# Eight-stage transformer kernel on one core: the wide attention's queries turned by VectorE 32x32 squares and a DRAM round trip instead of by TensorE, its probabilities divided on GpSimd, the narrow attention's copies moved to ScalarE, and a new order of steps

## Chip, cores and metric

One NeuronCore of a Trainium2 chip runs the whole program. The metric is device time in microseconds of one execution. All arithmetic the prediction speaks of is float32, except where a shape says f16 or bf16.

## What is computed

Four layers over x of 16x128x256, that is 16 blocks of 128 rows (context 128 rows of 128 a block), each layer a cross-attention and a feed-forward part, both added to x after a layer norm:

```python
x = x + _L0_xattn_ref(ln(x), ...)   # 32 heads of 8, rotary angles         -> stage 0
x = x + _L0_ffn_ref(ln(x), ...)     # product-key expert retrieval          -> stage 1
x = x + _L1_xattn_ref(ln(x), ...)   # 16 heads of 128, masked, grouped      -> stage 2
x = x + _L1_ffn_ref(ln(x), ...)     # 7 routed experts and a shared one     -> stages 3, 8, 9
x = x + _L2_xattn_ref(ln(x), ...)   # 16 heads of 16, two softmaxes, biases -> stage 4
x = x + _L2_ffn_ref(ln(x), ...)     # ternary weights                       -> stage 5
x = x + _L3_xattn_ref(ln(x), ...)   # 16 heads of 128, normed q and k       -> stage 6
x = x + _L3_ffn_ref(ln(x), ...)     # block-quantised weights and inputs    -> stage 7
```

The wide attention of layer 3 is `q = rmsnorm(x@Wq, gq); k = rmsnorm(ctx@Wk, gk); p = softmax(q k^T / sqrt(128)); out = (p v) @ Wo`, for 16 heads of 128.

## The kernel before

Every block of 128 rows passes through the steps listed in `STEPS`. Each step has a name, a number of repeats (4 in stage 6: four groups of four heads) and the engines that work on it (T TensorE, V VectorE, A ScalarE, G GpSimd, S the sync engine that issues DMAs). `ORDER` is a string per engine, one letter a step, that lays down by hand in which order the engine runs all its steps; the stages overlap at their borders, and stage 7 runs interleaved with stage 6, stage 1 with the end of stage 0, stage 5 with stage 4. Every engine works strictly in its order and waits on semaphores. Eight PSUM banks of 128x512 are handed round by `BANKS`.

Stage 6, per group of four heads (64 groups in all). TensorE: `q` (L1301, L1302) and `k` (L1308) project; `tq` (L1314) turns the four queries with four transposes into a PSUM bank; `sc` (L1323) makes scores; `pv` (L1329) and `wo` (L1337) follow. ScalarE: `q` copies the queries out of PSUM (L1644) and squares them (L1647), `k` squares the keys (L1652), `tq` copies the turned queries with the gain (L1658), `sc` is the exponential (L1673), `pv` a copy (L1664). VectorE: `nk`, `nq` sum the squares (L2313, L2319), `kn` scales the keys (L2324), `tk` turns them in 32x32 squares (L2333), `sc` takes the maximum (L2347) and scales it (L2351), `pn` takes the reciprocal of the sums (L2356) and multiplies the 128x512 probabilities by it (L2358), `pt` turns these in squares (L2341). GpSimd: the powers of -1/2 of `nk` and `nq` (L2564 to L2572), and one DMA each for `tk` (L2555) and `pt` (L2560), which writes the squares to DRAM. The sync engine then reads them back with four DMAs of 64 KB each, so placed that the squares land where a full 128x128 turn wants them (`turned_in`, L866). Keys and probabilities already take this way; queries don't. Stage 7 has VectorE steps on 128x1024 tiles (L2368 to L2420).

Stage 0: `split` makes the low halves of the f16 pairs with two subtractions on VectorE (L1867, L1868), while GpSimd duplicates the high halves (L2525, L2526); GpSimd also adds the rotary terms (L2520) and the output bias (L2515).

Stage 4: VectorE takes the turned keys out of PSUM with weight and bias (L1878, L1879), and the values with side mask and bias (L1899, twice a block); ScalarE takes the queries (L1451). A step `ms` interleaves on TensorE the maximum-squares of block b with the score-squares of block b-1 (L1016, L1012), two banks each; GpSimd raises the variances to -1/2 (L2533).

The way of keys and probabilities through DRAM, in the code:

```python
eng.dma_start(turn3k[n % 4], u6.Dk.rearrange("p (j w) -> p j w", j=4)).then_inc(S["l3_kw"], 16)   # GpSimd
src = mem.rearrange("(i r) j w -> i r j w", i=4)                                                   # sync engine
for j in range(4):
    eng.dma_start(to[32 * j:32 * j + 32].rearrange("r (i w) -> r i w", i=4), src[:, :, j, :].rearrange("i r w -> r i w")).then_inc(done, 16)
```

## Time and profile before

| | |
|---|---|
| time, median of 3 runs | 2078.17 us (2077.08 to 2088.37) |
| the profiled execution | 2088.02 us, its span 2085.8 us, mean granted TensorE clock 0.989 |
| busy, share of the span | TensorE 96%, weight loads 75%, VectorE 82%, ScalarE 61%, GpSimd 32% |
| chain that ended last | TensorE 53%, VectorE 29%, issue 7%, ScalarE 4%, GpSimd 4%, DMA 3% |

Busy is a union of recorded durations. Matmuls are pipelined and their records overlap, so a busy TensorE may still have room. The chain of waits is followed back from the last instruction, at each step to what released it. Lines of stage 6 are L1301 to L1337 (TensorE), L1644 to L1673 (ScalarE) and L2313 to L2358 (VectorE).

### The profile page before, as it was taken

How to read it: one execution, taken by the hardware profiler on the slowest of the kernel's cores; microseconds unless marked ns; L12 is line 12 of the kernel's file. 1: busy time of each engine (PE TensorE's matmuls, PEld its weight loads, DVE VectorE, ACT ScalarE, POOL GpSimd, SP SyncE). 2: the span in 40 equal slices, each digit the busy share in tenths (PEclk: the TensorE clock that was granted, in tenths of full speed). 3: DMA queues.
4: the chain of work that ended last, by engine and by line, in shares of the span. 5: the costliest groups of instructions: out<-in, count | busy, mean ns of one | idle time of the engine just before them, and what ended most of it. 6: DMA issues, size and time to landing. Idle time of an engine off the chain costs nothing.

```text
span 2085.8 us, 46042 instructions
## 1 busy us (share of the span) xinstructions
PE 1997.6 (96%) x16294; PEld 1564.6 (75%) x16294; DVE 1713.2 (82%) x4655; ACT 1274.0 (61%) x3214; POOL 667.7 (32%) x1000
## 2 busy tenths in 40 slices
PE   5999899999999999998998889999999999999998
PEld 3666799999988888877997667887665666656665
DVE  7887899999689997766447789896887998888877
ACT  3778988798944554544653444634766666567552
POOL 6321020000012232222128776111665345434420
PEclk8999999999999999999999899999999999999999
DMA  9400300000045443433220010023544233333320
GB/s 336 144 3 2 124 6 2 2 2 2 12 151 168 137 151 104 142 102 89 89 65 26 29 62 2 2 87 122 166 150 133 91 112 114 127 105 107 122 81 25
DMA packets 181515, 182.28 MB, mean 87 GB/s; under 512 B 20678, under 2 KB 160088, under 8 KB 180264
## 3 DMA queue, kind: packets, MB, share of 16 engines
q1 hardware_dynamic: 160168, 112.49, 17.5%
q0 software_dynamic: 21120, 66.87, 8.8%
q8 instruction: 130, 2.13, 0.4%
q14 instruction: 97, 0.79, 0.1%
HBM read 99.06 MB, written 80.22 MB: 86 GB/s over the span
## 4 chain that ended last, share of the span: by engine, by line
PE 53%; DVE 29%; issue 7%; ACT 4%; POOL 4%; DMA 3%; SPq 1%; another core or an unknown queue 0%; DVEq 0%; ACTq 0%; POOLq 0%
PE pb L1141 4%; PE pb L1164 3%; PE pb L1274 3%; PE pb L1337 2%; PE pb L1042 2%; PE pb L1149 2%; PE pb L1376 2%; PE pb L1359 2%; PE pb L1222 2%; PE pb L1360 2%; PE pb L1156 2%; PE pb L1283 2%; PE pb L995 2%; PE pb L1213 2%; PE pb L1329 1%
## 5 line engine op out<-in xcount | busy, mean ns | idle before, releaser
L2472 POOL TENSOR_SCALAR sm<-sm 128x1 f32<-128x1 f32 x128 | 33.7, 263 | 455.9 <-DVE sm L1745 454.9
L1508 ACT ACTIVATE areaB<-i128h,workB 128x128 f16<-128x128 f16 x512 | 156.2, 392 | 0.1
L1465 ACT ACTIVATE areaA<-pb 128x512 f32<-128x512 f32 x192 | 106.8, 600 | 61.6 <-PE pb L1012 35.2
L1535 ACT ACTIVATE workA<-workA 128x128 f32<-128x128 f32 x256 | 99.4, 390 | 60.8 <-DVE workA L2059 55.5
L1673 ACT ACTIVATE workA<-pb,workA 128x128 f32<-128x128 f32 x256 | 113.9, 460 | 30.9 <-DVE workA L2351 30.3
L1097 PE MATMUL pb<-areaB 128*128 128x128 f32 x1024 | 126.7, 280 | 3.1 <-ACT workB L1498 2.9
L1141 PE MATMUL pb<-xT,areaA 128*128 128x128 f32 x1024 | 124.2, 276 | 0.0
L1097 PEld LDWEIGHTS pb<-areaB 128*128 128x128 f32 x1024 | 119.8, 194 | 5.6 <-ACT workB L1498 3.3
L1141 PEld LDWEIGHTS pb<-xT,areaA 128*128 128x128 f32 x1024 | 120.0, 192 | 4.5 <-issue 4.0
L1164 PE MATMUL pb<-areaA,workA 128*128 128x256 f32 x512 | 121.6, 382 | 0.9 <-ACT workA L1542 0.9
L1337 PE MATMUL pb<-areaA,workA 128*128 128x256 f32 x512 | 120.7, 380 | 0.0
L2541 POOL DMA_DIRECT2D turn<-workA x64 | 37.1, 580 | 245.3 <-DVE workA L2072 244.8
L1113 PE MATMUL pb<-areaB,workB 128*128 128x256 f32 x512 | 113.7, 380 | 1.1 <-DVE workB L2036 1.1
L1337 PEld LDWEIGHTS pb<-areaA,workA 128*128 128x128 f32 x512 | 95.0, 190 | 25.3 <-issue 12.9
L1164 PEld LDWEIGHTS pb<-areaA,workA 128*128 128x128 f32 x512 | 93.8, 190 | 21.6 <-issue 8.5
L1113 PEld LDWEIGHTS pb<-areaB,workB 128*128 128x128 f32 x512 | 96.0, 190 | 13.9 <-DVE workB L2036 1.3
L1887 DVE TENSOR_REDUCE workA<-pb 128x4 f16<-128x512 f32 x128 | 83.4, 689 | 13.9 <-PE pb L995 13.5
L1042 PE MATMUL pb<-areaA,workA 128*32 128x128 f32 (+1 forms) x1536 | 86.4, 285 | 5.3 <-ACT areaA L1465 4.3
L2533 POOL TENSOR_TENSOR areaA<-areaA,neghalf 128x32 f32<-128x32 f32 x16 | 87.6, 5475 | 1.3
L1323 PEld LDWEIGHTS pb<-workA 128*128 128x128 f32 x512 | 65.1, 191 | 21.7 <-issue 18.6
L2474 POOL TENSOR_TENSOR sm<-sm,neghalf 128x1 f32<-128x1 f32 x128 | 76.7, 599 | 10.7
L1664 ACT COPY workA<-pb 128x512 f32<-128x512 f32 x64 | 37.8, 590 | 66.5 <-PE pb L1329 66.0
(426 smaller groups left out, 5872.0 us busy)
## 6 DMA issues: line engine op xcount, KB each, us to landing
turn<-workA POOLq DMA_DIRECT2D x64, 256.0 KB
workA<-turn SPq DMA_DIRECT2D x256, 64.0 KB
turn3k<-areaA POOLq DMA_DIRECT2D x64, 256.0 KB, 2.7
workA<-turn3k SPq DMA_DIRECT2D x256, 64.0 KB, 2.0
turn3p<-areaA POOLq DMA_DIRECT2D x64, 256.0 KB, 2.7
rows_in<-areaB SPq DMA_DIRECT2D x7, 2048.0 KB, 16.5
areaA<-turn3p SPq DMA_DIRECT2D x168, 64.0 KB, 2.0
workA<-turn3p SPq DMA_DIRECT2D x88, 64.0 KB, 2.0
```

The lines of the kernel that those rows point to most:

```text
L1042: m = eng.matmul(p[r, k * 128:(k + 1) * 128], vt[:, h, :], P[:, j * 128:(j + 1) * 128], start=True, stop=True)
L1097: m = eng.matmul(p[:, e * 128:(e + 1) * 128], w.ed[:, k, (4 * c + e) * 128:(4 * c + e + 1) * 128], xT[:, k, :], start=(k == 0), stop=(k == 1))
L1113: m = eng.matmul(p[:, 0:256], G[:, e, :], w.eu[:, e, :], start=(e == 0), stop=(e == 15))
L1141: m = eng.matmul(p[:, h * 128:(h + 1) * 128], w.wq[:, 4 * c + h, k], xT[:, k, :], start=(k == 0), stop=(k == 1))
L1164: m = eng.matmul(p[:, 0:256], u.OT[i][:, h], w.wo[:, 4 * c + h], start=(c == 0 and h == 0), stop=(c == 3 and h == 3))
L1337: m = eng.matmul(p[:, 0:256], u.OT[i][:, h], w.wo[:, 4 * c + h], start=(c == 0 and h == 0), stop=(c == 3 and h == 3))
L1465: eng.activation(u.P[n % RP], bank(*held)[:, :], ACT.Exp, scale=1.0 / math.sqrt(hd)).then_inc(freed(*held)[0], 1)
L1508: m = eng.activation(u.far[:, g], i128h[:, :], ACT.Square, bias=u.at[b % 2][:, 8 * c + g:8 * c + g + 1])
L1535: m = eng.activation(u.P[i][:, h], u.P[i][:, h], ACT.Exp, accum_out=u.den[i][:, h:h + 1], bias=u.nm[i][:, h:h + 1])
L1673: m = eng.activation(u.P[i][:, h], p[:, h * 128:(h + 1) * 128], ACT.Exp, accum_out=u.den[i][:, h:h + 1], bias=u.nb[i][:, h:h + 1], scale=u ...
L1887: eng.tensor_reduce(o[:, :, 24:25], p, AX.X, ALU.max, negate=True).then_inc(freed(s, tag, b, c // 2)[0], 1)
L2533: eng.tensor_tensor(va, va, neghalf[:, 0:32], ALU.pow).then_inc(S["l2_rs"], 1)
```

## The change

- Stage 6, queries: TensorE's `tq` and ScalarE's copy (L1644) go. VectorE turns the queries in squares straight from PSUM; GpSimd writes them to DRAM with one DMA; the sync engine reads them back with four; ScalarE applies the gain from SBUF; `sc` waits for that. ScalarE's square of the queries now waits for VectorE's squares, and `q` alternates between two banks (0 and 3).
- Stage 6, probabilities: VectorE keeps the reciprocal, GpSimd multiplies the 128x512 tile.
- Stage 0: the two subtractions of `split` run on GpSimd, behind its copies.
- Stage 4: ScalarE takes the turned keys and the values; the value bias leaves that step and is added, both sides summed, in `oT`, which becomes two activations with bias instead of a copy. `ms` is split into `mx` and `st`, each over four row groups and the same four banks (3 to 6); TensorE's matmuls are the same.
- `ORDER` is new for all five engines. The stages overlap about as before: at its last step of stage 0 VectorE has 33 steps of stage 1 behind it, where it had 24; at the last step of stage 5 it has 16 of stage 6, where it had 14.

The core of the diff (the order strings, names of semaphores, buffers of stage 4 and the host's preparation of the bias are left out):

```diff
-    0: (("lnA", 1, "VG"), ("lnB", 1, "VG"), ("xT", 1, "TA"), ("qk", 1, "T"), ("rope", 1, "VG"), ("split", 1, "AVG"),
+    0: (("lnA", 1, "VG"), ("lnB", 1, "VG"), ("xT", 1, "TA"), ("qk", 1, "T"), ("rope", 1, "VG"), ("split", 1, "AG"),
-        ("nc", 1, "V"), ("tqk", 1, "TAV"), ("vp", 1, "TV"), ("ms", 2, "T"), ("mxr", 4, "V"), ("tq2", 1, "TA"),
-        ("ex", 4, "A"), ("pv", 4, "T"), ("ot", 2, "A"), ("tb", 2, "T"), ("norm", 2, "V"), ("oT", 1, "TA"),
+        ("nc", 1, "V"), ("tqk", 1, "TA"), ("vp", 1, "TA"), ("mx", 1, "T"), ("mxr", 4, "V"), ("tq2", 1, "TA"),
+        ("st", 1, "T"), ("ex", 4, "A"), ("pv", 4, "T"), ("ot", 2, "A"), ("tb", 2, "T"), ("norm", 2, "V"), ("oT", 1, "TA"),
-    6: (("lnA", 1, "VG"), ("lnB", 1, "V"), ("xT", 1, "TA"), ("k", 4, "TA"), ("nk", 4, "VG"), ("kn", 4, "V"), ("q", 4, "TA"),
-        ("nq", 4, "VG"), ("tq", 4, "TA"), ("tk", 4, "VGS"), ("sc", 4, "TVA"), ("pn", 4, "V"), ("pt", 4, "VGS"),
+    6: (("lnA", 1, "VG"), ("lnB", 1, "V"), ("xT", 1, "TA"), ("k", 4, "TA"), ("nk", 4, "VG"), ("kn", 4, "V"), ("q", 4, "TVA"),
+        ("nq", 4, "VG"), ("tq", 4, "GSA"), ("tk", 4, "VGS"), ("sc", 4, "TVA"), ("pn", 4, "VG"), ("pt", 4, "VGS"),
...
-    (6, "q"): lambda b, c: (("q", 0),),
+    (6, "q"): lambda b, c: (("q", (0, 3)[c % 2]),),
-        u6.qn = [carve(512) for _ in range(2)]
+        u6.Dq = [carve(512) for _ in range(2)]
         u6.qT = [carve(512).rearrange("p (h n) -> p h n", n=128) for _ in range(2)]
+        u6.qr = [work[1][:, 8704 + 512 * k:9216 + 512 * k] for k in range(2)]
         u6.kT = [carve(512) for _ in range(2)]
...
+                elif (s, step) == (6, "tq"):
+                    n = 4 * b + c
+                    d.wait_ge(S[f"l3_qw{n % 2}"], 16 * (n // 2 + 1))
+                    if n >= 2:
+                        d.wait_ge(S["l3_qg"], n - 1)
+                    turned_in(turn3q[n % 4], u6.qr[n % 2], S[f"l3_qr{n % 4}"])
...
+                    rows = range(2 * (c % 2), 2 * (c % 2) + 2) if s == 0 else range(4)
+                    tags = [step + "ab"[i % 2] if s == 0 else f"{step}{i}" for i in rows]
+                    p = [room(s, tag, b, c) for tag in tags]
...
-                elif step == "tq":
-                    t.wait_ge(S["l3_qn"], nth(b, c, 4))
-                    p = room(6, "tq", b, c)
-                    for h in range(4):
-                        m = eng.transpose(p[:, h * 128:(h + 1) * 128], u.qn[i][:, h * 128:(h + 1) * 128], ident)
-                    m.then_inc(full(6, "tq", b, c)[0], 1)
...
+                        if step == "tqk":
+                            a.wait_ge(*full(4, "tk", b))
+                            src, dst = bank(4, "tk", b)[:, :].rearrange("p (t n) -> p t n", n=128), u.kT[b % RQ]
+                            eng.activation(dst[:, :, 0:112], src[:, :, 0:112], ACT.Identity, scale=w4.nwc[:, 1:2], bias=w4.nwc[:, 4:5])
+                            eng.activation(dst[:, :, 112:128], src[:, :, 112:128], ACT.Identity, scale=w4.nwc[:, 2:3],
+                                           bias=w4.nwc[:, 5:6]).then_inc(freed(4, "tk", b)[0], 1)
...
+                    src = bank(4, "v", b)[:, 0:256].rearrange("p (h e) -> p h e", e=16)
+                    for k in range(2):
+                        m = eng.activation(u.vt[b % RV][:, :, 17 * k:17 * k + 16], src, ACT.Copy, scale=side[k])
...
+                        for k in range(2):
+                            m = eng.activation(u.OT[b % 2][:, k], src[:, k], ACT.Identity, bias=w4.bsum[:, k:k + 1])
...
                 elif step == "q":
                     a.wait_ge(*full(6, "q", b, c))
-                    p = bank(6, "q", b, c)
-                    if two:
-                        a.wait_ge(*full(6, "tq", *two))
-                    eng.copy(u.qn[i], p[:, :]).then_inc(S["l3_qn"], 1)
+                    a.wait_ge(S["l3_qt"], nth(b, c, 4))
                 elif step == "tq":
-                    a.wait_ge(*full(6, "tq", b, c))
+                    n = 4 * b + c
+                    a.wait_ge(S["gp_done"], 1)
+                    a.wait_ge(S[f"l3_qr{n % 4}"], 64 * (n // 4 + 1))
-                    a.wait_ge(S["gp_done"], 1)
-                    eng.activation(u.qT[i], bank(6, "tq", b, c)[:, :].rearrange("p (h n) -> p h n", h=4), ACT.Copy,
-                                   scale=gp[:, 0:1]).then_inc(freed(6, "tq", b, c)[0], 1)
+                    eng.activation(u.qT[i].rearrange("p h (i w) -> p h i w", i=4),
+                                   u.qr[i].rearrange("p (i h w) -> p h i w", i=4, h=4), ACT.Copy, scale=gp[:, 0:1]).then_inc(S["l3_qg"], 1)
...
-                    eng.tensor_tensor(qp[:, 0, :, 8:16], y4[:, 0], qp[:, 0, :, 0:8], ALU.subtract)
-                    eng.tensor_tensor(qp[:, 1, :, 16:24], y4[:, 1], qp[:, 1, :, 0:8], ALU.subtract).then_inc(S["l0_split"], 1)
...
-                        eng.tensor_scalar(dst[:, :, 0:112], src[:, :, 0:112], w.nwc[:, 1:2], w.nwc[:, 4:5], ALU.mult, ALU.add)
-                        eng.tensor_scalar(dst[:, :, 112:128], src[:, :, 112:128], w.nwc[:, 2:3], w.nwc[:, 5:6], ALU.mult,
-                                          ALU.add).then_inc(freed(4, "tk", b)[0], 1)
-                    for k in range(2):
-                        m = eng.scalar_tensor_tensor(vt[:, :, 17 * k:17 * k + 16], src, side[k], w.bvs[k], ALU.mult, ALU.add)
...
+                if step == "q":
+                    n = 4 * b + c
+                    v.wait_ge(*full(6, "q", b, c))
+                    if n >= 2:
+                        v.wait_ge(S[f"l3_qw{n % 2}"], 16 * (n // 2))
+                    eng.transpose(u.Dq[n % 2].rearrange("p (j h w) -> p h j w", j=4, h=4),
+                                  bank(6, "q", b, c)[:, :].rearrange("p (h j w) -> p h j w", h=4, j=4)).then_inc(S["l3_qt"], 1)
...
-                    eng.reciprocal(u.rec[i], u.den[i]).then_inc(*v.mark())
-                    v.settle()
-                    eng.tensor_tensor(u.P[i], u.P[i], bc(u.rec[i], 2, [128, 4, 128]), ALU.mult).then_inc(S["l3_pn"], 1)
+                    eng.reciprocal(u.rec[i], u.den[i]).then_inc(S["l3_rec"], 1)
...
+                    eng.tensor_tensor(qp[:, 0, :, 8:16], y4[:, 0], qp[:, 0, :, 0:8], ALU.subtract)
+                    eng.tensor_tensor(qp[:, 1, :, 16:24], y4[:, 1], qp[:, 1, :, 0:8], ALU.subtract).then_inc(S["l0_split"], 1)
...
-                if step == "tk":
+                if step == "tq":
+                    g.wait_ge(S["l3_qt"], n + 1)
+                    if n >= 4:
+                        g.wait_ge(S[f"l3_qr{n % 4}"], 64 * (n // 4))
+                    eng.dma_start(turn3q[n % 4], u6.Dq[n % 2].rearrange("p (j w) -> p j w", j=4)).then_inc(S[f"l3_qw{n % 2}"], 16)
...
+                elif step == "pn":
+                    g.wait_ge(S["l3_rec"], nth(b, c, 4))
+                    P, rec = u6.P[c % 2], u6.rec[c % 2]
+                    eng.tensor_tensor(P, P, bc(rec, 2, [128, 4, 128]), ALU.mult).then_inc(S["l3_pn"], 1)
```

## Rows read from the trace of the kernel before

**Rows 1.** Windows of the whole trace: length, busy of each engine, granted clock, DMA share
```profile
0.00:52.00 52.00, 29.14 (x228) 19.39 (x229) 38.44 (x99) 16.08 (x29) 35.06 (x67) 0.87 0.99 336
52.00:208.00 156.00, 153.47 (x2500) 105.06 (x2500) 129.89 (x278) 121.42 (x225) 36.20 (x68) 1.00 0.15 50
208.00:572.00 364.00, 353.99 (x3827) 329.89 (x3828) 328.52 (x1419) 313.06 (x752) 29.94 (x57) 1.00 0.06 21
...
1096.00:1300.00 204.00, 179.91 (x1909) 143.29 (x1909) 167.72 (x461) 88.66 (x172) 150.40 (x134) 0.94 0.10 30
...
1445.00:1560.00 115.00, 110.95 (x495) 71.80 (x493) 88.16 (x183) 81.21 (x217) 69.40 (x113) 1.00 0.51 166
1560.00:2030.00 470.00, 461.36 (x1877) 295.81 (x1876) 400.82 (x763) 295.96 (x734) 200.51 (x321) 1.00 0.35 111
```

**Rows 2.** Chain that ended last: the whole span, then 208 to 572, then 1445 to 1560
```profile
PE 53%; DVE 29%; issue 7%; ACT 4%; POOL 4%; DMA 3%; SPq 1%; another core or an unknown queue 0%; DVEq 0%; ACTq 0%; POOLq 0%
...
by line: DVE workB L1946 7.6%; DVE workB L2036 7.5%; PE pb L1097 7.2%; DVE workB L2027 7.2%; DVE areaB L2027 6.8%; DVE workB L1940 6.0%; PE pb L1113 5.7%; DVE workB L2018 4.6%; issue 4.2%; DVE workB L1960 3.4%; DVE workB L1976 3.4%; DVE wor
...
by line: DMA turn3k<-areaA 10.9%; PE pb L1337 10.0%; issue 7.8%; PE pb L1329 5.9%; PE pb L1301 5.5%; PE pb L1302 5.3%; DMA turn3p<-areaA 5.1%; POOL workA L2566 4.4%; PE pb L1323 4.4%; SPq L866 3.6%; DVE areaA L2333 3.0%; POOL workA L2572 2.
```

**Rows 3.** Query turn: its group of lines, then the timeline of TensorE
```profile
L1314 PE MATMUL pb<-cst,workA 128*128 128x128 f32 x256 | 38.5, 273 | 1.5 <-ACT workA L1658 1.0 <-ACT xT L1422 0.4
...
1710.11 0.60 PE L1314 MATMUL pb<-cst,workA 128*128 128x128 f32 x4
1710.55 1.02 PE L1329 MATMUL pb<-areaA,workA 128*128 128x512 f32 x2
1711.41 1.02 PE L1308 MATMUL pb<-areaA,ctxT 128*128 128x512 f32 x2
```

**Rows 4.** Groups of lines of stages 6 and 7 on ScalarE and VectorE
```profile
L1658 ACT ACTIVATE workA<-pb,gp 128x512 f32<-128x512 f32 x64 | 44.6, 696 | 22.1 <-PE pb L1314 22.1
...
L2333 DVE STREAM_TRANSPOSE areaA<-workA 128x512 f32<-128x512 f32 x64 | 45.1, 704 | 11.5 <-DMA turn3k<-areaA 9.1 <-ACT areaA L1637 1.9
...
L2358 DVE TENSOR_TENSOR workA<-workA 128x512 f32<-128x512 f32 x64 | 44.5, 696 | 2.2
...
L2387 DVE TENSOR_TENSOR workB<-workB 128x1024 f32<-128x1024 f32 x16 | 19.5, 1220 | 0.3
```

**Rows 5.** GpSimd groups, DMA issues with landing, and the sync queue's timeline
```profile
L2555 POOL DMA_DIRECT2D turn3k<-areaA x64 | 38.7, 605 | 56.4 <-DVE areaA L2333 55.6 <-issue 0.4
...
L2520 POOL TENSOR_TENSOR workA<-workA 128x512 f32<-128x512 f32 x16 | 20.6, 1286 | 9.0 <-DVE workA L1868 5.4 <-DVE workA L1823 3.7
...
turn3k<-areaA POOLq DMA_DIRECT2D x64, 256.0 KB, 2.7
workA<-turn3k SPq DMA_DIRECT2D x256, 64.0 KB, 2.0
...
1701.72 1.80 SPq L866 DMA_DIRECT2D workA<-turn3k  x4
```

**Rows 6.** Windows of L2566 alone, once a head group
```profile
1445.00:1560.00 115.00, 17.47 (x17) 1.00 0.51 166
1560.00:2030.00 470.00, 49.46 (x46) 1.00 0.35 111
```

**Rows 7.** Timelines of VectorE and GpSimd where both read SBUF twice
```profile
23.33 1.48 DVE L1867 TENSOR_TENSOR workA<-workA 128x256 f16<-128x256 f32 x1
...
23.21 1.31 POOL L2520 TENSOR_TENSOR workA<-workA 128x512 f32<-128x512 f32 x1
...
1713.40 2.01 POOL L2566 TENSOR_TENSOR workA<-workA,neghalf 128x4 f32<-128x4 f32 x1
```

**Rows 8.** Line L1867, durations min/median/max, the first of two alike
```profile
L1867 DVE TENSOR_TENSOR workA<-workA x16: 415/421/1484, 23.3 to 189.9; 128x256 f16<-128x256 f32 x16
```

**Rows 9.** Groups of lines of stage 4, window 1092 to 1340
```profile
L1899 DVE SCALAR_TENSOR_TENSOR workA<-pb,cst,areaA 128x256 f32<-128x256 f32 x32 | 13.9, 475 | 0.2 <-PE pb L962 0.2
...
L1878 DVE TENSOR_SCALAR workA<-pb,areaA 128x448 f32<-128x448 f32 x16 | 11.8, 737 | 2.6 <-PE pb L979 2.6
```

## Prediction before the change was timed

> **What bounds the kernel now.** The windows by stage come first [rows 1]. TensorE is busy 461 of 470 us in the long mix of stages 6 and 7 (1560 to 2030), 111 of 115 in the head of stage 6 (1445 to 1560), 153 of 156 in stage 0 after its start, 354 of 364 in stage 1, but 180 of 204 in stage 4 (1096 to 1300), where its granted clock averages 0.94 and not 1.00, so some of it ran at 1.2 and not 2.4 GHz. VectorE is second everywhere: 90% in stage 1 (328.5 of 364), 82% in stage 4, 77% in the head of stage 6, 85% in the mix. GpSimd matters in three places: the start (35 of 52), stage 4 (150 of 204) and the head of stage 6 (69 of 115).
>
> Busy TensorE time overstates its need, because matmul records overlap, so the chain of waits comes second [rows 2]. TensorE holds 53% of it, VectorE 29%. From 208 to 572 the named lines are mostly VectorE's: stage 1 goes by VectorE. In the head of stage 6 the largest piece is the landing of the keys' squares in DRAM, 10.9%, with 5.1% for the probabilities', 4.4% for GpSimd's power and 3.6% for the sync queue. So the reader should see three limits: VectorE in stage 1, a mixture in stage 4, and in stage 6 TensorE with DRAM round trips close behind.
>
> All sums are against the profiled execution, 2088.02 us (span 2085.8, 2.2 around it). It stands 9.85 us above the median of 2078.17; I take the difference off the result.
>
> **Stage 6, queries: what TensorE saves.** The group of the query turn shows 38.5 us for 256 transposes [rows 3], but these are overlapping records. In the timeline the four transposes start at 1710.11 and the next step at 1710.55: a step advances TensorE by 0.44 us. 64 x 0.44 = 28.2 us. That is the saving if TensorE bounds; 38.5 is not, and it is the upper bound only if the 0.16 us tails are real room too.
>
> **What it costs elsewhere, per group of heads.** VectorE gains one square turn: that of the keys, from SBUF, takes 0.704 us [rows 4]; from PSUM no such turn is in the trace. Bounds: the advance of about 0.60 between pipelined operations of this size (not lower, it streams as many elements) and twice 0.704; I take 0.704, since it is the same operation and size. VectorE loses the multiplication, 0.696 [rows 4]. Over 64 groups +45.1 - 44.5: nothing. ScalarE loses one copy of 128x512 and keeps the gain copy, 0.696 from PSUM, now from SBUF [rows 4]: at most 45 us less on an engine at 63% in the mix, worth nothing by itself. GpSimd gains a DMA issue, 0.605 [rows 5], and the multiplication. A GpSimd operation with two tensor inputs of 128x512 took 1.286 us [rows 5], against VectorE's 0.696, so 1.29. Together 1.89 x 64 = 121 us more GpSimd. The sync engine gains four DMAs, 1.80 us for the four [rows 5], 115 us in all; DMA traffic gains 64 x 0.5 MB = 33.6 MB.
>
> Beside what does this lie? In the mix there are 46 groups in 470 us [rows 6], 10.2 us a group; GpSimd goes from 200.5 to 200.5 + 46 x 1.89 = 287 us of 470, and it is covered. In the head there are 17 groups in 115 us, 6.8 us each: GpSimd goes from 69.4 to 69.4 + 17 x 1.89 = 101.5 of 115, 88%, in order and with six visits a group. There it is nearly the bound, and I give back the head's whole share of the saving, 17 x 0.44 = 7.5 us. The sync engine's 17 x 1.80 = 31 us on top of 17 x 3.6 = 61 fit into 115; the DMA share would go from 0.51 to about 0.74 (33.6 x 17/64 = 8.9 MB in 115 us is 78 GB/s on 166).
>
> The way of the queries lengthens. Before, a copy out, turn 0.44, gain copy 0.70: 1.8 us with 0.70 for the first copy as well. After, 0.70 squares, 0.61 issue, 2.7 to land, 1.8 for the four reads, 2.0 to land [rows 5], 0.70 gain: 8.5 us. In the new order string of TensorE the steps between `q` 9.2 and its `sc` are `hT`, `q`, `k`, `sc`, `out`, `k`: a step of 512 columns (`k`, `sc`) advances TensorE by 1711.41 - 1710.55 = 0.86 [rows 3], `q` is two such, `out` four, `hT` two turns of 0.44, so they last 0.9 + 1.7 + 0.9 + 0.9 + 3.4 + 0.9 = 8.7 us; between `q` 9.0 and its `sc` some 14. So it is covered in the mix, with next to no slack at the tightest. If this cover goes, the late thing is `sc`, and behind it every later TensorE step, since it is in order.
>
> **What two engines do to each other.** At 23.33 VectorE's subtraction with two SBUF inputs took 1.48 us, 0.42 by its line's median [rows 7, 8]; GpSimd's two-input add had begun at 23.21 and ended at 24.52. Conversely GpSimd's power took 2.01 us at 1713.40, under VectorE's two-input multiplications of stage 7. Whoever starts first makes the other wait. The Trainium skill says why, on the page GPSIMD Engine Reference, sections Key points and Engine selection: GpSimd shares its SBUF interfaces with VectorE, with contention for operations with two SBUF inputs, and elementwise work with two inputs belongs on VectorE, GpSimd being about twice as slow; the trace agrees with both (1.286 against 0.696, 1.48 against 0.42). Followed to the end that rule speaks against moving the multiplication. The price: each of 64 multiplications can hold VectorE up by at most 1.48 - 0.42 = 1.06 us, 68 us in all, at least nothing. VectorE uses such operations in about a quarter of the mix (in stage 7 four of 1.22 us a block [rows 4], and smaller ones, of some 40 us), so I take one in eight of the bound as net loss of time: 3 us after cover in the mix, because VectorE has 69 us of room there [rows 1].
>
> Stage 6 and 7 in all: -28.2 + 7.5 + 3 = about -18.
>
> **Stage 0.** Two subtractions of 0.42 a block leave VectorE: 13 us [rows 8]. They join GpSimd, which shows no such subtraction; for 256 elements between half of 1.286 and 1.286, 0.7 taken, 1.4 a block, and 22 us on an engine at 36 of 156 us. After the start TensorE bounds stage 0, so nothing is gained there; a block's turn waits about 1 us longer, covered by blocks in flight. What may be gained is VectorE work of stage 1 done earlier: it has 9 more steps of stage 1 behind it, and stage 1 then goes by VectorE [rows 2]. These are three steps of `ae`, three of `am`, two of `gm` and one of `lnB`, of 0.4 to 0.7 us a piece: 4 us. In the start, where GpSimd has 35 of 52 us, it is as likely to lose 3 us as the lifted collision of rows 7 is to gain 2. I take -4 for stages 0 and 1, from +4 (GpSimd late in the start) to -12 (nearly all 13 us).
>
> **Stage 4.** VectorE loses, a block, 2 x 0.475 + 0.737 us and a small copy beside the second, whose columns are a seventh of its neighbour's and which I price at 0.2 to 0.7, 0.3 taken: 2.0 us, 32 us in all [rows 9], of 168 busy in 204. ScalarE gains as much or a little more, 35 us on 89 of 204. TensorE's matmuls stay. Its room is 24 us by the record of busy time [rows 1], and the clock's 0.94 means another 12 of 204. VectorE holds a third of the time on the way here, so of 32 us a quarter: -8. Bounds: 0 or +5 (four banks shared by `mx` and `st`, so that the next block's `mx` waits for the exponentials; keys behind queries on ScalarE, about 1 us later a block) to -20. The bias step itself moves inside the load of weights: nothing.
>
> **Sum.** -18 - 4 - 8 = -30: 2058 for the profiled execution, 2048 against the median.
>
> **Rivals.** (1) *The queries' way through DRAM sets the pace; slower.* Place: `sc` in all 64 groups. The keys' landing has 10.9% of the head's chain, 12.5 us for 17 groups, 0.74 us a group; with the sync queue's and GpSimd's part (18.9%, 21.7 us) 1.28 us. If the queries pay the same everywhere, they cost 47 to 82 us against 28 + 12 saved: +7 to +42, middle 2100. It decides from 0.63 us a group on. For it: 8.5 us against a cover of 8.7, and three users of one sync queue and one GpSimd queue. Against: in the mix the keys' landing is rare among the longest pieces. 13%.
> (2) *VectorE and GpSimd lock each other.* If most multiplications cost VectorE the full 1.06 us, VectorE goes from 401 to 450 of 470 in the mix, and the 20 us that TensorE saves there are gone; stages 0 and 4 keep -12: 2066 to 2074. This is where the skill's rule leads if the cover isn't there. 17%.
> (3) *The new order also closes gaps.* TensorE sits idle by record 4 us in the head, 9 in the mix, 24 in stage 4, 10 in stage 1. With all of 28, -20 in stage 4 and -12 in stages 0 and 1: -60, 2018; as a case 2012 to 2035. 20%.
> (4) The turned queries were filling holes that stay as holes: TensorE's busy time falls, the end hardly moves, 2068 to 2078. This is the change not doing what it says; for it, TensorE has only 53% of the chain. It is counted inside (2).
>
> **How the numbers follow.** Forecast 50% (2035 to 2062), rivals 13, 17 and 20%. About 0.5%, 10.4 us, is what a measurement of this kernel can tell. Faster: the forecast, rival 3 and a third of rival 2: 0.75. Same: the rest of rival 2 and a little of rival 1: 0.13. Slower: 0.12. The range takes in rival 3 down to its -60 and rival 2 whole, and leaves out most of rival 1: 2016 to 2084.
>
> **What would show it.** Right: the stretch from the first line of stage 6 to the end falls from 641 us to 615 to 630; L2358's kin appears on GpSimd at 1.3 us, some at 2; VectorE's turn from PSUM near 0.70; GpSimd at 85 to 90% in the head; stage 4 shorter by 5 to 12 us with VectorE below 75%. Wrong: landings of the queries' squares among the first of the chain, TensorE's score step waiting for ScalarE's gain copy, or VectorE's two-input operations with medians well above 1.22 us.

## The result, and the profile after

| | before | after |
|---|---|---|
| median of the runs beside each other | 2080.3 us (9 runs, 2075.52 to 2088.37) | 2072.56 us (9 runs, 2066.55 to 2075.8) |
| ratio after to before | | 0.9959, 95% interval 0.9948 to 0.9971 |
| profiled execution, its span | 2088.02 us, 2085.8 us | 2073.72 us, 2071.8 us |
| stages 4 and 5: last `up` matmul of the shared expert (L1240, after: L1234) to the last matmul of stage 5 (L1283, after: L1277) | 1107.1 to 1445.7, 338.6 us | 1112.1 to 1431.8, 319.7 us |
| stage 6 and 7: first query step to the end | 1446.9 to 2085.8, 638.9 us | 1433.0 to 2071.8, 638.8 us |

The change makes the kernel 0.4% faster, 7.7 us by the medians, less than the 0.5% that the prediction took as what can be told; it had said 30. The interval excludes 1, so the small gain is real. The last two rows say where: the gain lies in stages 4 and 5, and none in stages 6 and 7, where the queries' turn left TensorE. The two profiled executions overstate it with 14 us between them: that of the kernel before stands 7.7 us above its median, that of the kernel after 1.2 above its own. (The recorded expectations measure stages 4 and 5 from rows that merge several steps, about 1 us shorter: 337.5 there is 338.6 here.) The chain that ended last in the kernel after:

```profile
PE 50%; DVE 24%; POOL 8%; issue 7%; DMA 5%; ACT 3%; SPq 3%; DVEq 0%; POOLq 0%; ACTq 0%
```

Its windows, columns as in [rows 1]: stages 0 and 1, stage 4, the head of stage 6, the mix (the last two shifted by the 14 us that stage 6 begins earlier), then stages 6 and 7 whole.

```profile
52.00:208.00 156.00, 153.31 (x2469) 106.85 (x2466) 118.78 (x248) 120.11 (x223) 49.02 (x93) 0.98 0.15 48
208.00:572.00 364.00, 355.70 (x3875) 331.10 (x3875) 332.11 (x1426) 313.76 (x761) 30.91 (x58) 1.00 0.07 22
...
1096.00:1300.00 204.00, 187.04 (x2115) 154.39 (x2114) 158.48 (x449) 125.36 (x263) 163.46 (x145) 0.97 0.11 32
...
1431.00:1546.00 115.00, 102.20 (x410) 61.48 (x409) 86.61 (x177) 70.07 (x192) 84.53 (x134) 1.00 0.70 228
1546.00:2016.00 470.00, 450.31 (x1712) 278.21 (x1711) 410.63 (x768) 286.26 (x703) 275.68 (x424) 1.00 0.53 167
...
1433.00:2071.80 638.80, 600.55 (x2297) 371.22 (x2295) 538.39 (x1004) 368.56 (x918) 362.19 (x560) 1.00 0.52 167
```

The same stretch (stages 6 and 7 whole) of the kernel before:

```profile
1446.90:2085.80 638.90, 620.62 (x2553) 399.16 (x2551) 531.39 (x1008) 391.30 (x978) 271.26 (x436) 1.00 0.35 114
```

TensorE had 18 idle us in these 639 by record and now has 38: the work left, the time did not. In the head TensorE is busy 102 of 115 us, where it was 111 [rows 1]. VectorE does as much as before (531 and 538), GpSimd a third more (271 to 362), DMA half as much again (0.35 to 0.52). In the chain TensorE gives way, 53% [rows 2] to 50%, and GpSimd, DMA and the sync queue come up, 8 + 5 + 3% where they had 4 + 3 + 1.

The groups of the moved work, stages 6 and 7 of the kernel after (L2301 and L2333: VectorE's turns of the queries and of the probabilities; L2562: the division on GpSimd; L2548: the issue of the queries' write):

```profile
L2301 DVE STREAM_TRANSPOSE workA<-pb 128x512 f32<-128x512 f32 x64 | 44.9, 702 | 4.1 <-PE pb L1296 4.0
L2333 DVE STREAM_TRANSPOSE areaA<-workA 128x512 f32<-128x512 f32 x64 | 44.8, 700 | 15.9 <-DMA turn3p<-areaA 8.7 <-POOL workA L2562 6.9
...
L2562 POOL TENSOR_TENSOR workA<-workA 128x512 f32<-128x512 f32 x64 | 67.4, 1055 | 18.0 <-DVE workA L2348 17.3
L2548 POOL DMA_DIRECT2D turn3q<-workA x64 | 39.1, 610 | 52.4 <-DVE workA L2301 49.2 <-issue 3.0
```

So single prices were near or on the safe side: the turn from PSUM takes 0.702 us (0.704 taken), the division 1.055 (1.29 taken), the issue 0.61. GpSimd is busy 74% of the head of stage 6 (84.53 of 115 us), where 88% was forecast. Waits of the same stretch, in total, times, longest:

```profile
ACT workA L1665 <- DMA workB<-turn3q: 54.2, 38, 3.3
...
PEld pb L1311 <- ACT workA L1665: 20.5, 20, 2.2
...
PE pb L1311 <- ACT workA L1665: 9.4, 13, 1.5
```

and of the sync engine's own queue:

```profile
SPq L873 <- DMA turn3p<-areaA: 95.0, 32, 8.3
SPq L873 <- DMA turn3q<-workA: 63.8, 23, 10.8
```

ScalarE's gain copy (L1665) waits for the landing of the turned queries in 38 of 64 groups. TensorE's scores (L1311) wait for the gain copy, 29.9 us in 33 waits of their weight loads and matmuls: the sign that the prediction named for being wrong. And the sync engine stands 63.8 us before reads of queries whose write hasn't landed, with the reads of keys and probabilities queued behind. From the start of VectorE's turn (L2301) to the end of the gain copy the queries' way takes 11.4 us in the median group, 7.6 in the fastest and 20.4 in the slowest. Two theories follow. **A**: the queries' way through DRAM, with its places in two queues, took what TensorE gave. **B**: VectorE and GpSimd hold each other up in the division (VectorE's operations that overlap it ran over their usual time, the median of their line, by about 16 us in all).

### The profile page after: what moved, and what is told of

It reads as the page before. It is cut to its first block, busy times and chain, and to the rows that moved or that the text cites. A ratio compares the mean times of both kernels' runs of the same rounds, so it can differ in the third digit from the quotient of the medians.

```text
span 2071.8 us, 46041 instructions
## 1 busy us (share of the span) xinstructions
PE 1968.2 (95%) x16038; PEld 1533.0 (74%) x16038; DVE 1684.7 (81%) x4558; ACT 1276.6 (62%) x3230; POOL 779.6 (38%) x1160
## 4 chain that ended last, share of the span: by engine, by line
PE 50%; DVE 24%; POOL 8%; issue 7%; DMA 5%; ACT 3%; SPq 3%; DVEq 0%; POOLq 0%; ACTq 0%
PE pb L1135 3%; PE pb L1268 3%; PE pb L1158 3%; PE pb L1107 3%; PE pb L1091 3%; PE pb L1036 3%; PE pb L1009 3%; SPq L873 2%; PE pb L1216 2%; PE pb L1143 2%; PE pb L1150 2%; PE pb L1207 2%; PE pb L1277 2%; PE pb L1100 1%; DMA turn3k<-areaA 1%
## 5 line engine op out<-in xcount | busy, mean ns | idle before, releaser
L1544 ACT ACTIVATE workA<-workA 128x128 f32<-128x128 f32 x256 | 99.5, 390 | 64.0 <-DVE workA L2044 63.8
L1469 ACT ACTIVATE areaA<-pb 128x512 f32<-128x512 f32 x192 | 104.9, 603 | 28.7 <-PE pb L1009 28.2
L1311 PEld LDWEIGHTS pb<-workA 128*128 128x128 f32 x512 | 64.8, 191 | 39.0 <-ACT workA L1665 20.5
L1009 PE MATMUL pb<-workA 32*128 32x128 f16 (+2 forms) x2048 | 83.8, 255 | 7.5 <-DVE workA L1881 4.1
L1009 PEld LDWEIGHTS pb<-workA 32*128 32x128 f16 (+2 forms) x2048 | 59.7, 142 | 37.2 <-issue 25.4
L1036 PE MATMUL pb<-areaA,workA 128*32 128x128 f32 (+1 forms) x1536 | 81.9, 286 | 4.5 <-ACT areaA L1469 3.7
```

The lines of the kernel that those rows point to most:

```text
L1009: m = eng.matmul(p[k][:, j * 128:(j + 1) * 128], one, two, start=True, stop=True)
L1036: m = eng.matmul(p[r, k * 128:(k + 1) * 128], vt[:, h, :], P[:, j * 128:(j + 1) * 128], start=True, stop=True)
L1469: eng.activation(u.P[n % RP], bank(s, tag, b, at)[:, :], ACT.Exp, scale=1.0 / math.sqrt(hd)).then_inc(freed(s, tag, b, at)[0], 1)
L1544: m = eng.activation(u.P[i][:, h], u.P[i][:, h], ACT.Exp, accum_out=u.den[i][:, h:h + 1], bias=u.nm[i][:, h:h + 1])
```

## The experiments

The runs were timed in five groups, each on one chip beside the kernel before, and ratios are within the group. The groups differ: the kernel before took 2078.5 us in the first (e1 to e4), 2087.9 in the second (e5, e6, e9), 2080.9 in the third (e10 to e13), 2081.5 in the fourth (e14 to e17) and 2089.3 in the fifth (e18 to e20). A second measure is steadier: the length of the last stretch, from the first query step to the end, in the profile. Four profiles of the kernel before give 637.3 to 638.9, two of the kernel after 638.8 and 638.6.

Two limits of these measures. A difference between ratios of two groups is known to about 5 us only. And the stretch is one execution's; where TensorE's granted clock falls to the lower of its two levels (0.50 of 2.4 GHz), up to half of that time is lost. The traces show this for 13.7 us of the last stretch in e1 and in e5, 6.8 in e3 and in e18, 20.5 in e19, 3.4 in e11 and in e14 and 116 in e15, and for under 1 us in the others, the kernels before and after among them.

| run | what it is | time, us (median) | ratio to before (95%) | last stretch, us |
|---|---|---|---|---|
| e9_before_again | before | 2087.7 | 0.9993 (0.9980 to 1.0007) | 638.8 |
| e17_before_third | before, one execution | 2084.5 | | 637.3 |
| e20_before_fourth | before, one execution | 2078.8 | | 638.3 |
| e13_after_again | after | 2072.4 | 0.9956 (0.9940 to 0.9973) | 638.6 |
| e1_pn_vector | after, division on VectorE | 2079.1 | 0.9997 (0.9985 to 1.0010) | 652.7 |
| e2_no_trip | no trip of the queries | 2052.9 | 0.9875 (0.9861 to 0.9889) | 619.9 |
| e3_no_trip_pn_vector | both | 2067.4 | 0.9944 (0.9931 to 0.9957) | 637.0 |
| e4_old_6_7 | stages 6 and 7 as before | 2074.2 | 0.9980 (0.9972 to 0.9989) | 641.0 |
| e5_no_latency | trip issued, not waited for | 2083.3 | 0.9978 (0.9966 to 0.9990) | 647.7 |
| e6_one_read | one plain read, not four | 2075.0 | 0.9936 (0.9917 to 0.9955) | 636.7 |
| e10_writes_only | half the trip | 2060.4 | 0.9897 (0.9877 to 0.9916) | 629.6 |
| e11_reads_only | the other half | 2056.5 | 0.9872 (0.9851 to 0.9893) | 624.1 |
| e12_write_scalar | whole, writes by ScalarE | 2072.5 | 0.9956 (0.9937 to 0.9976) | 640.9 |
| e14_no_turn | no trip, no turn of the queries at all | 2041.9 | 0.9814 (0.9790 to 0.9838) | 610.0 |
| e15_reads_later | whole, reads a place later | 2193.3 | 1.0545 (1.0521 to 1.0569) | 765.8 |
| e16_write_only_scalar | half the trip, by ScalarE | 2051.4 | 0.9866 (0.9841 to 0.9890) | 620.5 |
| e18_pn_gpsimd_old | old stages 6 and 7, division on GpSimd | 2096.0 | 1.0040 (1.0025 to 1.0055) | 660.3 |
| e19_pn_gpsimd_later | and a later turn behind it | 2115.1 | 1.0125 (1.0096 to 1.0153) | 678.2 |

**The division back on VectorE.** Expected:

> The changed kernel, with only the division of the probabilities put back on VectorE, in the same place of the same order. Theory A (the queries' way through DRAM, with its work in the queues of GpSimd and the sync engine, took the place of TensorE's turn): GpSimd loses 64 x 1.05 = 67 us and VectorE gains 64 x 0.70 = 45 us, the trip stays, so the time stays within 8 us of the changed kernel, 2065 to 2080. Theory B (VectorE and GpSimd hold each other up in the multiplication): the 16 us of stretched VectorE operations go and the time falls by 10 us or more, to 2062 or below.

```diff
-                    eng.reciprocal(u.rec[i], u.den[i]).then_inc(S["l3_rec"], 1)
+                    eng.reciprocal(u.rec[i], u.den[i]).then_inc(*v.mark())
+                    v.settle()
+                    eng.tensor_tensor(u.P[i], u.P[i], bc(u.rec[i], 2, [128, 4, 128]), ALU.mult).then_inc(S["l3_pn"], 1)
...
-                elif step == "pn":
```

The whole gain of the change goes (ratio 0.9997), and the last stretch grows by 13.9 us. By the ratios the loss is 8 to 9 us, and this profile was taken of the slowest of the twelve executions (2085.8 against a median of 2079.1): up to 6.8 of its 13.9 us are the clock's. Theory B is out: the division on GpSimd is a gain, collisions included. A's range holds for the median, but what it overlooked is the point: 45 us of VectorE's work are worth 8 to 14 us. VectorE's busy time in the stretch rises by 26 us only (538.4 to 564.5), which fits 44.4 us of divisions less the 16 of stretched operations.

**Without the trip.** The gain copy reads VectorE's squares where they stand, which leaves out the exchange of blocks through DRAM. Expected:

> The changed kernel, with the queries' squares read by ScalarE's gain copy straight from the buffer that VectorE wrote (four buffers in turn); it leaves out the exchange of blocks through DRAM: 64 writes by GpSimd and 256 reads by the sync engine. VectorE's turn and GpSimd's division stay. Theory A: the 28 us that TensorE was freed of appear, a part of them at least: 2045 to 2058. Theory B: the trip is hidden, the locks stay, the time moves by less than 5 us: 2067 to 2077.

```diff
+                    if n >= 4:
+                        v.wait_ge(S["l3_qg"], n - 3)
+                    eng.transpose((u.Dq + u.qr)[n % 4].rearrange("p (j h w) -> p h j w", j=4, h=4),
...
-                                   u.qr[i].rearrange("p (i h w) -> p h i w", i=4, h=4), ACT.Copy, scale=gp[:, 0:1])
+                                   (u.Dq + u.qr)[n % 4].rearrange("p (i h w) -> p h i w", i=4, h=4), ACT.Copy, scale=gp[:, 0:1])
```

The last stretch falls to 619.9: the trip costs 18.8 us, 0.29 us a group; the ratios say 17. A holds. The trace also shows where the cost falls, since the order of steps is the same. The score step of the seventeenth group begins 124.5 us after the first query step in the kernel after and 116.6 us here, that of the last group 579.0 and 560.3. So the first 16 groups pay 7.9 us and the other 48 pay 10.8.

**Both.** Expected:

> Both edits together: no exchange of the queries through DRAM, division on VectorE. Theory A: about as without the exchange alone, 2043 to 2060, VectorE's 45 us more being covered or costing a little. Theory B: only the division's part shows, 2055 to 2065, the same as with the division alone moved back. If both limit in turn, this run lies below each of the two by 5 us or more.

637.0 us. The division on VectorE costs 17.1 us without the trip (up to 3.4 of them the clock's; 14.6 by the medians of the same group) and 13.9 with it. The two costs nearly add, so neither covers the other. The case in which this run lies below both others didn't come true: it is the division moved back that costs, and A's 2043 to 2060 missed that.

**Old stages 6 and 7 behind the new 0 to 5.** All code and order of stages 6 and 7 from the kernel before, each part at the place in its queue that it had there, counted by its neighbours. Expected:

> Stages 0 to 5, 8 and 9 of the changed kernel, with their new order, and stages 6 and 7 as they were before, code and order. The traces put the whole gain ahead of stage 6 (from the first query step to the end 638.9 us before, 638.8 after). If that is so, this kernel takes the time of the changed one, 2068 to 2076. If the new stages 6 and 7 do gain and the two profiled executions hid it, it takes 2078 or more.

2074.2 us, ratio 0.9980, with 641.0 us in the last stretch: within the 2068 to 2076 expected. By the ratio it stands 4 to 5 us behind the kernel after, of which 2.3 are its longer last stretch. Its own 4.2 us of gain and the 2.7 by which its last stretch is longer than that of before put 7 of the 8 to 9 us ahead of stage 6.

**What of the trip costs.** Expected of the trip that is issued but not waited for (buffers in turn of three, two extra waits that keep it ordered), and of one plain read in place of four:

> The changed kernel with the whole trip still issued and moved (64 writes, 256 reads, same bytes), but with nobody reading what lands: the gain copy takes VectorE's buffer, so the exchange of blocks is left out and only the waiting for it is gone. Without the trip at all the time was 2052.9, with it 2072.6. Theory L (latency: ScalarE's gain copy waits for the landing): 2053 to 2060. Theory Q (places in the two queues and DMA traffic, which delay the keys' and the probabilities' trips): 2066 to 2073.

> The changed kernel with the queries read back by one plain transfer of 2 KB lines in place of four of 512 byte pieces; it leaves out the exchange of blocks, the bytes and the wait for the landing stay. The sync engine issues 64 DMAs for the queries and not 256, some 1.3 us less a group. Theory Q with the sync queue as its place: 2056 to 2064. Theory L, or GpSimd's queue as the place: 2067 to 2073, since the landing is at most 1.3 us earlier.

```diff
-                    turned_in(turn3q[n % 4], u6.qr[n % 2], S[f"l3_qr{n % 4}"])
+                    eng.dma_start(u6.qr[n % 2].rearrange("p (j w) -> p j w", j=4), turn3q[n % 4]).then_inc(S[f"l3_qr{n % 4}"], 16)
```

The first is inconclusive: 647.7 us is worse than the whole trip, but the waits that it had to add show in its profile with 27.4 us in the sync queue (for the reads before, which land in the same buffer) and 8.0 us on GpSimd. Up to 6.8 us more are the clock's. It decides nothing between the two theories. The second moves the stretch by 2.1 us and the ratio to 0.9936, 2067 on the scale of the first result and so the foot of the range for a cost that does not lie in the sync engine's issues: 192 fewer issues of 0.45 us are hardly it.

> The changed kernel with only the first half of the queries' trip: GpSimd issues its 64 writes, nothing is read back, and the gain copy takes VectorE's buffer (four in turn); the exchange of blocks is left out. From the first query step to the end the changed kernel takes 638.8 us and the one without the trip 619.9. Theory G (GpSimd's place in its queue, 64 x 0.62 = 40 us more of it): 630 to 639 us for that stretch, the whole kernel within 8 us of the changed one. Theory S (the sync queue, whose reads stand behind landings): 620 to 626, 13 us or more below the changed one.

> Only the second half: the sync engine issues the 256 reads, of a table that lies ready in DRAM, as soon as VectorE has turned the squares, and waits for no landing of a write; GpSimd issues nothing, and the gain copy takes VectorE's buffer (three in turn). The exchange of blocks is left out. Theory S with the issue time of 1.8 us a group as its cost: 630 to 639 us. Theory S with the waiting for the written squares as its cost (63.8 us of waits for them in the sync queue, with the keys' and the probabilities' reads behind): 620 to 626, and as little for the writes alone, since the two halves meet only in the full trip.

Writes alone: 629.6, 9.7 us above no trip. Reads alone, of a table that lies ready, with no landing to wait for: 624.1, 4.2 us. Together 13.9 of 18.8; the other 4.9 come only when both halves are there and a read waits for its write. The writes alone lie next to theory G's range. The reads alone lie in that of theory S with the waiting as the cost, but that theory wanted as little for the writes, and they cost more. The split rests on one profile for each half: by the ratios the writes cost 5 us and the reads nothing, each to within 5. Who pays for the writes:

> The kernel with the queries' writes alone, nothing read back and the gain copy from VectorE's buffer (the exchange of blocks is left out), with the writes issued by ScalarE (0.33 us each) and not by GpSimd (0.62). With GpSimd the stretch took 629.6, without any trip 619.9. If GpSimd's queue is the cost: 620 to 623. If it is the traffic, or VectorE's wait for the landed write: 627 to 631.

> The changed kernel, whole and complete, with the queries' squares written to DRAM by ScalarE's queue, right behind ScalarE's squares of the same group, and not by GpSimd's. Theory G: GpSimd loses 40 us and some waits, the stretch from the first query step to the end falls to 628 to 635. Theory S: within 3 us of 638.8, or a little more, since ScalarE pays the issue.

```diff
                     eng.activation(u.sqq, bank(6, "q", b, c)[:, :], ACT.Square).then_inc(freed(6, "q", b, c)[0], 1)
+                    n = 4 * b + c
+                    if n >= 4:
+                        a.wait_ge(S[f"l3_qr{n % 4}"], 64 * (n // 4))
+                    eng.dma_start(turn3q[n % 4], u.Dq[n % 2].rearrange("p (j w) -> p j w", j=4)).then_inc(S[f"l3_qw{n % 2}"], 16)
```

Issued by ScalarE, the writes alone cost nothing (620.5 against 619.9, with the same bytes; the ratios differ by 6 us from those of GpSimd's writes). So here the writes' traffic is free, and the cost of the writes alone was their place in GpSimd's queue. But in the whole kernel the same edit brings nothing, 640.9 against 638.8, with the same ratio, as theory S had it. GpSimd is relieved (325 us busy, not 362), and the wait for the landings stays:

```profile
ACT workA L1669 <- DMA workB<-turn3q: 53.1, 35, 4.3
```

53.1 us of waits of the gain copy, where the kernel after has 54.2. With the writes off GpSimd and the reads free of waits the two parts would come to 0.6 + 4.2, some 625 us; measured are 640.9, so what is left, about 16 us by this subtraction, is the waiting for written squares. No run separates the gain copy's own waiting from that of the reads queued behind in the sync engine. The costs don't add; each covers a part of the other.

> The changed kernel, whole and complete; in the sync queue 58 of the 64 reads of the queries stand one place later, behind the next read of keys or probabilities. If the reads that wait in front of others cost the time (61 to 64 us of waits of the sync queue for the written squares), the last stretch falls from 638.7 to 632 to 636 us. If it is the queries' own latency, it grows to 640 or more.

```diff
 S order, stage 6, one of 58 swaps
-tq(8.1) tk(8.2)
+tk(8.2) tq(8.1)
```

The first guess was wrong by far, and the second, the queries' own latency, holds: 765.8 us, 127 more. The sync queue's waits for written queries do fall, from 63.8 to 2.4 us, but those for the others rise (probabilities from 95.0 to 172.4, keys from 32.7 to 91.5), and the gain copy waits three times as long:

```profile
SPq L873 <- DMA turn3p<-areaA: 172.4, 44, 11.0
...
SPq L294 <- PE pb L1311: 72.4, 21, 9.1
...
SPq L873 <- DMA turn3q<-workA: 2.4, 2, 2.2
```

```profile
ACT workA L1665 <- DMA workB<-turn3q: 182.3, 49, 12.0
```

One place later puts 58 reads behind the landing of another write. It also closes a ring. The sync engine stands 72.4 us, 21 times, before a read whose buffer an earlier score (L1311) must free (9.3 us and 5 times in the kernel after), while scores wait for queries whose read now stands behind that one. A part is the clock, which falls to 0.92 in the last stretch: the same 2297 TensorE rows are busy 640.5 us, not 600.6, so some 40 of the 127 us are longer matmuls. So the queries' latency is no slack here. Whether another order would be better than the one the kernel has was not tried.

**Neither trip nor turn.** ScalarE makes the gain copy straight from PSUM; this leaves out the queries' turn altogether. Expected:

> The changed kernel with neither the trip nor VectorE's turn of the queries: ScalarE makes its gain copy straight from PSUM (four buffers in turn), and the whole turn of the queries is left out, on every engine. TensorE's order and work stay, VectorE loses 64 x 0.70 = 45 us. Without the trip alone the last stretch took 619.9 us. If VectorE sets the pace there: 600 to 611 us, and the prediction's zero for VectorE was the wrong step. If TensorE does: 616 to 621.

610.0 us, 9.9 less than without the trip. Last stretch and chain of that kernel:

```profile
1431.50:2041.50 610.00, 592.06 (x2297) 374.38 (x2295) 500.13 (x940) 361.99 (x918) 324.73 (x496) 1.00 0.37 120
```

```profile
PE 60%; DVE 22%; issue 6%; POOL 5%; ACT 3%; DMA 3%; SPq 1%; DVEq 0%; POOLq 0%; ACTq 0%
```

So VectorE's 45 us of turns cost 9.9 there (13 by the ratios), and the forecast's zero for them was wrong. In that figure is also the queries' shorter way, since the gain copy no longer waits for a turn. TensorE holds 60% of the chain and is busy 97% of the stretch. The steps from kernel to kernel are then: 638.3 before (mean of four profiles), less 28.3 to this kernel for the two reliefs together (the turn off TensorE, the division off VectorE, with the new order), plus 9.9 for VectorE's turns, plus 18.8 for the trip, 638.7 after. The sum closes by construction, being differences of measured stretches. No run shows TensorE's relief without VectorE's.

**The division on GpSimd in the old stages 6 and 7.** Its place in GpSimd's queue is where VectorE's reciprocal stood in time. Expected of this, and of the same with VectorE's turn of the probabilities one step later:

> Stages 0 to 5 as changed; stages 6 and 7 as before (queries turned by TensorE, old order), with one edit: GpSimd divides, its multiplication set into its queue where VectorE's reciprocal stood in time. With the division on VectorE this kernel took 2074.2, a ratio of 0.9980. Where TensorE sets the pace, 45 us less of VectorE are worth little: 0 to 5 us less. Where VectorE does, as the trip-less kernels show, 6 to 14 us less, 2060 to 2068, which would beat both kernels. Against it: VectorE's turn of the probabilities stands right behind the reciprocal in its queue and now waits for GpSimd, 1.05 us and more a group, which may make it slower by up to 20 us.

> The same, with VectorE's turn of the probabilities moved one step later in VectorE's queue, so that it does something else while GpSimd divides. If the wait behind the reciprocal matters, this run is faster than the one without the move, by up to 0.5 us a group, 10 to 30 us in all; if it doesn't, the same within 3 us.

660.3 us where the division on VectorE had 641.0, and 678.2 with the turn moved a step back (up to 3.4 and 10.3 us of it the clock's). The price came from where the first expectation put its doubt, but a step later for the turn is worse and not better; the cause of that stays open. Waits of the first:

```profile
POOL workA L2550 <- DVE workA L2341: 87.2, 28, 13.7
...
DVE areaA L2326 <- POOL workA L2550: 39.7, 41, 2.0
```

GpSimd stands 87.2 us before a division whose reciprocal isn't ready (17.3 in the kernel after), and VectorE's turn waits 39.7 us for it, 41 times (6.9 in the kernel after). In these two placements in the old queues the division's move costs, and in the new queues it gains; other placements were not tried. No version here beats the kernel after with the whole computation; the writes on ScalarE tie with it.

**The kernels unchanged.**

> The changed kernel, unchanged, beside the others of this call: chips differ by some us (the kernel before took 2078.5 in one call and 2087.9 in another), so the ratio to the kernel before may differ too. Expected: the ratio 0.996 again if the gain is the same on each chip, and 0.991 to 0.994 if this is the chip on which the kernel before takes 2088, where its stage 4 and 5 took 17 us more than the changed one's.

> The kernel before, unchanged, for a second profile: its first one took 2088, ten more than the median. The four traces with the new stage 4 show 317 to 321 us from the last expert matmul to the last step of stage 5, the first of before 337.5. If that is the change's own gain, this trace shows 335 to 339 too, and the time lies elsewhere; if a part of it was that one execution's, it shows 322 to 332, as the medians (new stages 0 to 5 with old 6 and 7: 4.3 us less) suggest.

> The kernel before, unchanged, for a third profile, on this chip. If its stages 4 and 5 take 337 us from the last expert matmul to the last step of stage 5 here too, the new stage 4 is worth 17 us everywhere, and something else in the stages 0 to 5 takes 10 back. If they take 322 to 332, the first two profiles of it showed a chip on which the old stage 4 is slower.

> The kernel before, unchanged, for its stage 4 on this chip: 332 to 337 us from the last expert matmul to the last step of stage 5 as in its three other profiles, or 321 to 326, which is what the medians ask for.

The kernel after gave 0.9956 again. The four profiles of the kernel before, on at least three chips, have 338.6, 338.2, 333.0 and 332.7 us from the last `up` matmul of the shared expert to the last matmul of stage 5; the sixteen with the new stage 4 lie between 317.8 and 324.3. So this stretch is shorter by 8 to 21 us, some 15 in the middle, while the medians allow 8 to 9 for the whole change. The traces show most of what lies between. The stretch before and after, with columns as in [rows 1] (the granted clock stands behind the last count of instructions):

```profile
1107.10:1445.70 338.60, 313.80 (x3690) 255.34 (x3689) 283.39 (x776) 157.42 (x307) 160.70 (x153) 0.96 0.12 39
...
1112.10:1431.80 319.70, 302.99 (x3691) 250.97 (x3690) 259.67 (x720) 182.81 (x383) 168.14 (x162) 0.98 0.12 40
```

TensorE spends 23.9, 23.9, 20.5 and 10.2 us of it at the lower clock level in the four profiles of the kernel before, 13.7 and 6.8 in the two of the kernel after; half of the difference of the means, the most that it can cost, is some 5 us. And the new order takes the last `up` later: the shared expert's last matmul follows it by 12.3 us in the kernel before and by 9.1 in the kernel after, which moves 3 us out of the stretch without saving them. An estimate from these figures is 15 - 5 - 3, some 7 us, near the medians and the 7 of the run with the old stages 6 and 7. How much of the clock's part the new stage 4 brings about, and how much is that of single executions, stays open.

## Why the prediction was wrong

**Stages 6 and 7, -18 forecast, 0 measured: here it failed.** In the terms of its sum, -28.2 + 7.5 + 3, the runs give -18.4 for the kernel without the trip (638.3 to 619.9) and +18.8 for the trip. Two steps were wrong.
- "That is the saving if TensorE bounds", 28.2 us taken whole, with VectorE at "+45.1 - 44.5: nothing". TensorE did not bound alone. The stretch gave 28.3 us only where VectorE had lost the division and not yet got the turns. The turns took 9.9 of it back. The division off VectorE was worth 8 to 17 by itself, which leaves TensorE's own turn 11 to 20 if the parts add, and no run shows it alone. VectorE at 85% of the mix [rows 1] was not beside the path but in it, at 0.2 to 0.4 us for each microsecond of its work. The prediction used such a factor in stage 4 ("a quarter") and not here.
- "So it is covered in the mix, with next to no slack at the tightest", for the queries' way. The 7.5 us given back in the head were of the right size (7.9 over the first 16 groups), though not for the reason named, since GpSimd was busy 74% and not 88% there. The zero for the mix was 10.8 us over the other 48 groups. The way was priced at 8.5 us, as if each queue stood free, and took 11.4 in the median group, up to 20.4, with waits in GpSimd's and the sync engine's queues on it.

That 2072.6 us lies inside the range of 2016 to 2084 is no merit of the sum: the range reaches far beyond the forecast on both sides.

**Collisions, +3 forecast.** GpSimd's division does stretch VectorE's work. Timeline of VectorE in the kernel after, and of GpSimd beside it:

```profile
1942.87 2.41 DVE L2379 TENSOR_TENSOR workB<-workB 128x1024 f32<-128x1024 f32 x1
```

```profile
1943.13 1.05 POOL L2562 TENSOR_TENSOR workA<-workA 128x512 f32<-128x512 f32 x1
```

2.41 us for an operation of 1.22, 1.19 more, while GpSimd's multiplication runs its usual 1.05. Some 20 such events add up to 16 us of VectorE's time, and at VectorE's worth of 0.2 to 0.4 that is 3 to 6 us, more than covered by the 45 us that left. The 3 us of the forecast agree, partly by luck: one in eight of the 68 us bound is 8.5, and the step from there to 3 has no working. "Whoever starts first makes the other wait" doesn't hold here. In the event shown VectorE had started first and was held all the same, as in four others, while 61 of GpSimd's 64 multiplications ran their usual time and the longest took 1.41 us. Nor were they only operations with two SBUF tensors: about a third were scaled by a constant or a column (`TENSOR_SCALAR`).

By the rule of the Trainium skill, page GPSIMD Engine Reference, section Engine selection, the multiplication belongs on VectorE; the trace agrees that it is slower on GpSimd (1.055 against 0.696 us), but in this kernel's order, with VectorE in the path, moving it was right (ratio 0.9997 with it on VectorE, 0.9956 with it on GpSimd).

**Stages 0 and 1, -4 forecast, 0 measured.** VectorE lost its 11 us in stage 0 (129.9 to 118.8) and did more in stage 1 (328.5 to 332.1), yet the last step of stage 1 begins at 581.5 us, at 579.9 before. Over all traces its last matmul begins at 584.3 to 587.8 us in the four of the kernel before and at 582.9 to 589.5 in the sixteen with the new stages 0 and 1, 0.8 us earlier in the mean. The range of +4 to -12 holds it. What the earlier work ran into was not tried by a run of its own.

**Stage 4, -8 forecast, -7 to -9 by the medians.** Direction, place and size held. In the window from 1096 to 1300 us VectorE falls from 82 to 78% (below 75% was named as the sign), ScalarE takes 37 us more, TensorE's idle time falls from 24 to 17 us, and the granted clock rises from 0.94 to 0.97. The mechanism is argued and not shown: no run separates the moved copies from the new order, from the four banks of `mx` and `st`, or from the clock, which in other profiles of the kernel before was 0.95 and 0.97 in that window. The zero for VectorE in stages 6 and 7 and the quarter here can't both be right, and the agreement of the -8 may be luck.

**The rivals.** The first (the trip sets the pace) had the right mechanism at less than half its own threshold, 0.29 of 0.63 us a group, so there is no slowdown. The second (locks) has its mechanism, at 16 us of VectorE's time and not 49, and is refuted as the cause by moving the division back. The third (the new order closes gaps) didn't show in stages 6 and 7. The fourth ("filling holes", 2068 to 2078) names the right time for the wrong reason: TensorE's time does come free and shows, together with VectorE's, where nothing takes it back (610.0 us). 13% for "same" was too little: where the second engine runs at 85% and the new path has 0.2 us of slack, more of the chance belonged to a saving that is given back.

## What to carry to other kernels

An engine that is 85% busy beside the one taken for the bound is no free place: price each microsecond moved to or from it, here at 0.2 to 0.4, and don't let equal and opposite moves cancel out of the sum before asking which of them the path pays for. A new trip through DRAM costs by its place in the in-order queues that it shares; price it by taking it out of the kernel, because its parts (writes 9.7, reads 4.2, together 18.8) don't add: moving the writes to another queue gave back all of their cost when they stood alone and nothing in the whole kernel. Where it lands is worth a look, too: most of this cost fell where the forecast had written "covered". A queue written by hand goes with the division of work for which it was written: 58 of 64 reads one place later cost 127 us, and a move of work into two places of the old queues 19 and 37. And look at the granted clock of a profile and at its rank among the executions before a difference of a few microseconds is read from it: one such execution made 8 to 9 us look like 14.

## What the runs showed of the hardware

A square turn of 128x512 fp32 by VectorE takes as long from PSUM as from SBUF, 0.702 and 0.700 us. GpSimd's multiplication of 128x512 by a broadcast 128x4 took 1.055 us, an addition of two full tensors of that size 1.29 [rows 5]; two subtractions of 256 elements a partition in stage 0 took 0.67 each. ScalarE's queue issues a 256 KB write in 0.33 us (e12), GpSimd's in 0.61. A VectorE operation that overlaps a GpSimd multiplication of 1.05 us can take 1.19 us longer, also when it started first. The medians of the kernel before differ by up to 11 us (0.5%) between the groups of runs, more than this change is worth: only ratios within a group could be used.
